# A perceiver block on one core: queries leave PSUM over both banks in one go, and a router's logits are made ahead of the norm they wait for

## The reference

```python
q = ln_lat @ Wq                                   # 16 heads of 64
kv = jnp.concatenate([xn, ln_lat], axis=1) @ Wkv
weight = jnp.einsum('bhld,bhnd->bhln', q * scale, k * scale)
weight = softmax(where(full_mask, weight, neg))   # mask in the second layer
return out @ Wout
...
logits = xf @ Wr.T + expert_bias                  # xf = rmsnorm(x1) * g2
rw = softmax(logits); topw, topi = top_k(rw, 2); topw = softmax(topw)
shared = _swiglu(xf, sW1, sW2, sW3)
specialist = einsum('te,etd->td', combine, eo)    # eo: 8 experts on xf
```

## Time and profile before

| | us |
|---|---|
| median of 3 runs | 2065.31 (2063.27 to 2069.19) |
| the profiled execution's own time | 2067.51 |
| its span in the trace | 2065.6 |
| PE busy | 1914.6 (93%) |
| DVE busy | 1682.6 (81%) |
| ACT busy | 1250.5 (61%) |
| POOL busy | 898.2 (43%) |

### The profile page before, as it was taken

One profiled execution on the slowest core, in us unless ns is written; L12 is line 12 of the kernel. 1 busy time (PEld: TensorE's weight loads), 2 busy tenths in 40 slices (PEclk: granted clock), 3 DMA queues, 4 the chain that ended last, 5 costly groups with the idle time before them and its releaser, 6 DMA issues. The chain is left out here.

```text
span 2065.6 us, 34989 instructions
## 1 busy us (share of the span) xinstructions
PE 1914.6 (93%) x12326; PEld 1037.9 (50%) x12326; DVE 1682.6 (81%) x3999; ACT 1250.5 (61%) x2237; POOL 898.2 (43%) x951
## 2 busy tenths in 40 slices
PE   7899999999999999899788999999999999998786
PEld 6444544444454544433656545454545454544585
DVE  6889889889989896699666788879797978786657
ACT  4466666665757666444244676867777777776312
POOL 5576565666666652088231424333232323232004
PEclk9899999999999999989998999999999999999898
DMA  4332222222222220132104011211121111110100
GB/s 140 89 105 65 70 67 68 67 68 68 73 73 68 51 67 1 48 115 89 40 1 126 14 38 39 50 39 38 39 59 36 41 39 39 38 30 1 29 1 10
DMA packets 148854, 110.53 MB, mean 54 GB/s; under 512 B 120892, under 2 KB 136232, under 8 KB 148680
## 3 DMA queue, kind: packets, MB, share of 16 engines
q1 hardware_dynamic: 148680, 108.31, 18.8%
HBM read 65.15 MB, written 14.29 MB: 38 GB/s over the span
## 5 line engine op out<-in xcount | busy, mean ns | idle before, releaser
L1260 DVE TENSOR_TENSOR x_p_lo<-x_psum,x_p_hi 128x512 f16<-128x512 f32 (+1 forms) x864 | 583.9, 682 | 110.6 <-ACT x_psum L1022 109.8
L1021 ACT ACTIVATE x_p_hi<-x_psum 128x512 f16<-128x512 f32 (+1 forms) x448 | 268.2, 599 | 260.3 <-PE x_psum L865 210.3
L1021 ACT ACTIVATE x_p_hi<-x_psum,x_bcol 128x512 f16<-128x512 f32 (+1 forms) x416 | 289.7, 696 | 153.9 <-PE x_psum L865 151.9
L891 PE MATMUL x_psum<-x_p_hi,x_x_both 128*128 128x512 f16 (+1 forms) x832 | 317.1, 381 | 30.4 <-DVE x_p_lo L1260 29.5
L863 PE MATMUL x_psum<-x_q,x_xT_both 128*128 128x512 f16 x832 | 316.3, 380 | 3.0 <-DMA x_q<-x_shift_rows 3.0
L892 PE MATMUL x_psum<-x_p_lo,x_x_both 128*128 128x512 f16 (+1 forms) x832 | 315.7, 379 | 0.0
L893 PE MATMUL x_psum<-x_p_hi,x_x_both 128*128 128x512 f16 (+1 forms) x832 | 315.6, 379 | 0.0
L865 PE MATMUL x_psum<-x_q,x_xT_both 128*128 128x512 f16 x832 | 315.6, 379 | 0.0
L864 PE MATMUL x_psum<-x_q,x_xT_both 128*128 128x512 f16 x832 | 315.6, 379 | 0.0
L1199 DVE CUSTOM_DVE_ANT_0 x_junk<-x_psum,x_brow 128x512 bf16<-128x512 f32 (+2 forms) x512 | 279.3, 584 | 8.8 <-PE x_psum L942 6.7
L1202 DVE TENSOR_REDUCE x_mx<-x_psum 128x1 f32<-128x512 f32 (+2 forms) x512 | 276.6, 583 | 2.2 <-PE x_psum L942 1.1
(11 more groups left out here) (486 smaller groups left out, 3609.8 us busy)
## 6 DMA issues: line engine op xcount, KB each, us to landing
x_x_both<-context_rows SPq DMA_DIRECT2D x32, 832.0 KB, 5.3
context_rows<-x_x SPq DMA_DIRECT2D x16, 832.0 KB, 3.5
x_raw<-in_ctx SPq DMA_DIRECT2D x16, 768.0 KB
ssm_c_row<-ssm_bc_rows SPq DMA_DIRECT2D x16, 512.0 KB, 4.2
ssm_b_wide<-ssm_bc_rows SPq DMA_DIRECT2D x7, 512.0 KB, 3.5
x_mrow<-in_mask_BxS_bk SPq DMA_DIRECT2D x16, 200.1 KB
x_Wkv<-in_L_xattn_Wkv SPq DMA_DIRECT2D x4, 512.0 KB, 5.3
x_xT_both<-context_rows SPq DMA_TRANSPOSE x96, 4.0
```

What stands on the lines that cost most here:

```text
L891: pe.matmul(out, v_hi, p_hi[r][rows, :], start=start, stop=False)
L1021: act.activation(p_hi[r][rows, :], score[r][rows, :], ACT.Exp, scale=SCORE_UNIT, **bias).then_inc(p_hi_ready, 1)
L1260: v.tensor_tensor(p_lo[r][rows, :], score[r][rows, :], p_hi[r][rows, :], ALU.subtract).then_inc(p_lo_ready, 1)
```

## The change

Two parts that do not touch each other.

In both attention loops a "q" item leaves `aux` as a whole: ACT waits for the item's second bank, then copies 512 columns twice instead of 256 columns four times; DVE subtracts 512 columns once instead of 256 twice. `aux_free` and `hi_ready` go up by two at the end, where they went up by one for each bank. PE's matmuls, their waits on `aux_free` and the table of items are as before.

In the expert block the turned tokens for the router come from `u`, before the norm: PE turns them in place of part of the idle work, ACT copies them times the weight vector, PE makes the logits there, and DVE multiplies the logits by the norm factor `r1` afterwards. The router's first exponential stands before `xf_hi`, the second behind it; the Silu table is loaded behind the second one instead of behind the attention's exponentials. DVE's top two come ahead of `xf_lo`, and `max_index` and the weights behind the first two `hidden`.

```diff
-                for bank in range(2):
-                    act.wait_ge(aux_ready, at.ready(item, bank))
-                    later, src = queries_part(a, bank, at.place(item), later_q, 1)
-                    act.activation(later, src, ACT.Copy, scale=Q_UNIT)
-                    high, src = queries_part(a, bank, at.place(item), q_hi, 0)
-                    act.activation(high, src, ACT.Copy, scale=Q_UNIT).then_inc(hi_ready, 1)
+                act.wait_ge(aux_ready, at.ready(item))
+                later, src = queries_part(a, at.place(item), later_q, 1)
+                act.activation(later, src, ACT.Copy, scale=Q_UNIT)
+                high, src = queries_part(a, at.place(item), q_hi, 0)
+                act.activation(high, src, ACT.Copy, scale=Q_UNIT).then_inc(hi_ready, 2)
...
-                    for bank in range(2):
-                        v.wait_ge(hi_ready, at.n * HI_PARTS + 2 * a + bank + 1)
-                        (hi, src), (lo, _) = (queries_part(a, bank, aux, q, 0) for q in (q_hi, q_lo))
-                        v.scalar_tensor_tensor(lo, src, Q_UNIT, hi, ALU.mult, ALU.subtract).then_inc(aux_free, 1)
+                    v.wait_ge(hi_ready, at.n * HI_PARTS + 2 * a + 2)
+                    (hi, src), (lo, _) = (queries_part(a, aux, q, 0) for q in (q_hi, q_lo))
+                    v.scalar_tensor_tensor(lo, src, Q_UNIT, hi, ALU.mult, ALU.subtract).then_inc(aux_free, 2)
...
-                keep_clock(pe, slot[1], ident, 28)
+                for g in range(GROUPS):
+                    pe.wait_ge(x1_ready, g + 1)
+                    for t in range(g * GT, (g + 1) * GT):
+                        ins = pe.transpose(slot[0][:, t * P:(t + 1) * P], u[:, t, :], ident[:, :])
+                    ins.then_inc(u_turned, 1)
+                keep_clock(pe, slot[1], ident, 8)
+                pe.wait_ge(uT_ready, GROUPS)
+                for t in range(NT):
+                    ins = pe.matmul(slot[2][:, t * NE:(t + 1) * NE], xfT[:, t * P:(t + 1) * P], WT[:, VR, DK:WR], start=True, stop=True)
+                ins.then_inc(lg_made, 1)
+                keep_clock(pe, slot[1], ident, 12)
...
-                    if g == GROUPS - 1:
-                        act.activation(warm[:, :], ident[:, 0:1], ACT.Silu)
...
+                for g in range(GROUPS):
+                    act.wait_ge(u_turned, g + 1)
+                    act.activation(xfT[:, g * GT * P:(g + 1) * GT * P], slot[0][:, g * GT * P:(g + 1) * GT * P], ACT.Copy, scale=vec[:, 1:2]).then_inc(uT_ready, 1)
+                act.wait_ge(rw_less, 1)
+                act.activation(rw[:, :, :], lg[:, :, :], ACT.Exp).then_inc(rw_exp, 1)
                 act.wait_ge(xf_turned, 1)
                 for c in range(2):
                     act.activation(xf_hi[:, 512 * c:512 * c + 512], psum[:, 6 + c, :], ACT.Copy, scale=vec[:, 1:2]).then_inc(xf_hi_ready, 1)
...
+                act.wait_ge(top_less, 1)
+                act.activation(col[1][:, :], col[0][:, :], ACT.Exp).then_inc(top_exp, 1)
+                act.activation(warm[:, :], ident[:, 0:1], ACT.Silu)
...
-                v.tensor_tensor(lg[:, :, :], logits, bias_r[:, :].unsqueeze(1).to_broadcast(wide), ALU.add).then_inc(lg_read, 1)
+                logits = slot[2][:, 0:NT * NE].rearrange("p (t e) -> p t e", e=NE)
+                v.tensor_tensor(lg[:, :, :], logits, r1.unsqueeze(2).to_broadcast(wide), ALU.mult).then_inc(lg_read, 1)
...
+                steps.link(v.tensor_tensor(lg[:, :, :], lg[:, :, :], bias_r[:, :].unsqueeze(1).to_broadcast(wide), ALU.add))
...
+                v.tensor_tensor(col[0][:, :], best[:, :, 1], best[:, :, 0], ALU.subtract).then_inc(top_less, 1)
...
+                hidden(0)
+                hidden(1)
                 for t in range(NT):
                     steps.mark(v.max_index(place[:, t, :], best[:, t, :], rw[:, t, :]))
```

More of the change, by code:

```diff
@@ L723, in wait_alone, with queries_part @@
         eng.wait_ge(sem, value)
-    def queries_part(a, bank, aux, q, k):
-        src = aux[:, 512 * bank:512 * bank + 512].rearrange("p (c h k l) -> p c h k l", h=2, k=2, l=L)[:, :, :, k, :]
-        c = (a % 2) * (NC_ // 2) + bank * (NC_ // 4)
+    def queries_part(a, aux, q, k):
+        src = aux.rearrange("p (c h k l) -> p c h k l", h=2, k=2, l=L)[:, :, :, k, :]
+        c = (a % 2) * (NC_ // 2)
         if k == 0:
-            dst = q[a // 2][0][:, c:c + NC_ // 4, :].rearrange("p c (h l) -> p c h l", l=L)
+            dst = q[a // 2][0][:, c:c + NC_ // 2, :].rearrange("p c (h l) -> p c h l", l=L)
         else:
-            dst = q[:, (a // 2) * HL + c * P:(a // 2) * HL + (c + NC_ // 4) * P].rearrange("p (c h l) -> p c h l", h=2, l=L)
+            dst = q[:, (a // 2) * HL + c * P:(a // 2) * HL + (c + NC_ // 2) * P].rearrange("p (c h l) -> p c h l", h=2, l=L)
         return dst, src
@@ L1655, in expert_block @@
         pT_ready_v = sem("pT_ready_v")
-        (xf_ready, xf_turned, xfT_ready, lg_made, lg_read, rw_less, rw_exp, top_less, top_exp, comb_ready) = (
-            sem(n) for n in ("xf_ready", "xf_turned", "xfT_ready", "lg_made", "lg_read", "rw_less", "rw_exp", "top_less", "top_exp", "comb_ready"))
+        (xf_ready, xf_turned, lg_made, lg_read, rw_less, rw_exp, top_less, top_exp, comb_ready) = (
+            sem(n) for n in ("xf_ready", "xf_turned", "lg_made", "lg_read", "rw_less", "rw_exp", "top_less", "top_exp", "comb_ready"))
         (up_made, gated_made, silu_ready, hid_ready, down_made, added, res_ready) = (
             sem(n) for n in ("up_made", "gated_made", "silu_ready", "hid_ready", "down_made", "added", "res_ready"))
+        u_turned, uT_ready = sem("u_turned"), sem("uT_ready")
         W_hi_ready, W_lo_ready, xf_hi_ready, xf_lo_ready, hid_hi_ready, hid_lo_ready = (
@@ L1810, in down @@
                     pe.wait_ge(hid_lo_ready, e + 1)
-                    if e == 1:
+                    if e == 0:
                         pe.wait_ge(lg_read, 1)
@@ L1830, in _ @@
                     expert(slot[1], GATED + e, gated_made)
[L1831 to L1836, removed]
+                    if e >= LATE:
                         down(e - LATE)
@@ L1878, in _ @@
                     act.activation(xf_hi[:, 512 * c:512 * c + 512], psum[:, 6 + c, :], ACT.Copy, scale=vec[:, 1:2]).then_inc(xf_hi_ready, 1)
-                for c in range(2):
-                    act.wait_ge(xf_lo_ready, c + 1)
-                    act.activation(xfT[:, 512 * c:512 * c + 512], psum[:, 6 + c, :], ACT.Copy, scale=vec[:, 1:2]).then_inc(xfT_ready, 1)
+                act.wait_ge(top_less, 1)
+                act.activation(col[1][:, :], col[0][:, :], ACT.Exp).then_inc(top_exp, 1)
+                act.activation(warm[:, :], ident[:, 0:1], ACT.Silu)
                 def high(e):
@@ L1892, in _ @@
                         high(1)
[L1893 to L1896, removed]
                     act.wait_ge(up_made, e + 1)
@@ L1966, in add @@
                     ins.then_inc(added, 1)
[L1968 to L1972, removed]
                 v.wait_ge(counted, 1)
@@ L1976, in _ @@
                 v.wait_ge(bias_in, 16)
-                logits = slot[3][:, 0:NT * NE].rearrange("p (t e) -> p t e", e=NE)
-                v.tensor_tensor(lg[:, :, :], logits, bias_r[:, :].unsqueeze(1).to_broadcast(wide), ALU.add).then_inc(lg_read, 1)
+                logits = slot[2][:, 0:NT * NE].rearrange("p (t e) -> p t e", e=NE)
+                v.tensor_tensor(lg[:, :, :], logits, r1.unsqueeze(2).to_broadcast(wide), ALU.mult).then_inc(lg_read, 1)
                 v.wait_ge(lg_read, 1)
+                steps.link(v.tensor_tensor(lg[:, :, :], lg[:, :, :], bias_r[:, :].unsqueeze(1).to_broadcast(wide), ALU.add))
                 steps.link(v.tensor_reduce(col[0][:, :], lg[:, :, :], AX.X, ALU.max))
                 v.tensor_tensor(lg[:, :, :], lg[:, :, :], col[0][:, :].unsqueeze(2).to_broadcast(wide), ALU.subtract).then_inc(rw_less, 1)
-                hidden(1)
                 v.wait_ge(rw_exp, 1)
@@ L1989, in _ @@
                 steps.wait()
+                v.tensor_tensor(col[0][:, :], best[:, :, 1], best[:, :, 0], ALU.subtract).then_inc(top_less, 1)
+                for c in range(2):
+                    v.wait_ge(xf_hi_ready, c + 1)
+                    v.scalar_tensor_tensor(xf_lo[:, 512 * c:512 * c + 512], psum[:, 6 + c, :], vec[:, 1:2], xf_hi[:, 512 * c:512 * c + 512],
+                                           ALU.mult, ALU.subtract).then_inc(xf_lo_ready, 1)
+                hidden(0)
+                hidden(1)
                 for t in range(NT):
                     steps.mark(v.max_index(place[:, t, :], best[:, t, :], rw[:, t, :]))
-                v.tensor_tensor(col[0][:, :], best[:, :, 1], best[:, :, 0], ALU.subtract).then_inc(top_less, 1)
                 steps.wait()
```

## The result

The changed kernel takes 2101.72 us (median of 4 runs, 2100.98 to 2103.39), the kernel before, run beside it, 2067.25 (2063.27 to 2071.01). The ratio is 1.0168, 95% interval 1.0146 to 1.0191: 34.5 us slower, where +30.5 and 2096 were forecast, with a range from 2082 to 2108. The two profiled executions differ by 2100.7 - 2065.6 = 35.1 us of span.

A forecast was written before the change was run, and what follows sets the result against it. PE was taken to bound the query stretches. New waits and later stretch ends in the loops, +38.7 us, and the expert block, -8.2, summed to +30.5 and a forecast of 2096 us, range 2082 to 2108.

The forecast's parts named there:

- What bounds the stretch: Query stretches of both loops: PE sets the pace, busy 9.47 and 10.00 of 10 us; ACT has 1 to 2 to spare.
- the margin of 0.6 per bank: Query items, kernel before: each bank is free some 0.6 us before PE wants it, and the change spends that.
- Rival 1: Query items: copies and subtraction free the banks in time, the wait never forms, 2057 us; chance 0.07.
- The size of a wait: Query stretches: PE waits 0.79 us for its first bank before the second, third and fourth item.
- The third wait without mask: Six unmasked stretches: 0.18 us of lateness is already there, so the third wait adds only 0.61.
- The end of a stretch: Behind each stretch's last item: the exponential starts 0.44 us later, and all of it reaches PE.
- The places ahead of the two loops: Ahead of both attention loops, where little else runs: between 0 and 0.8 us lost, taken as 0.4.
- rival 2: Rest of each pair in the loops: PE's later waits absorb the delay, about 2068 us, same time; chance 0.05.
- rival 3: Query stretches: PE's granted clock falls, one low stretch in each of 14 costs 22 us more, 2118; chance 0.06.
- The expert block: Expert block: -1.4 for table load and warm operation, +0.1 at the front, -6.9 at the fourth "gated"; -8.2 us.
- rival 4: Expert block: the front of its loop costs what the removed waits give, 2104 us; chance 0.82 together with the forecast.
- the chain from `max_index` to `comb`: Expert block, DVE: takes 2.84 us ahead of the third `hidden`, so the fourth "gated" starts 6.7 earlier.

The follow-up runs named there:

- The two half-merged kernels: Kernel before with only ACT's copies merged: 2096.55 us, ratio 1.0127; kernel before with only DVE's subtraction merged: 2085.13 us, ratio 1.0079.
- one step of shift: Kernel before with ACT's copies and DVE's subtraction of a query item one step later in their lists: 2058.85 us, ratio 0.9952.

## Why the prediction held, point by point

- *What bounds the stretch.* Right. PE set the pace, the margin of 0.6 per bank was real and was spent, and the saved ACT time bought nothing. ACT's busy time fell by 16 us where some 20 were forecast: four times 0.38 counts the overlaps of the copies twice. Rival 1 (the wait never forms) fails by the 42 waits. The rule beside it is that of larger tiles (the Trainium skill, "Advanced Engine Details and Errata", section "The Read-Write Bubble"). It did save ACT time (597 ns for 512 columns, 384 for 256), but on an engine that waits. The other rule is that breaking up an instruction can let the work end sooner where an engine isn't saturated but causes gaps on others (the Trainium skill, "Perfetto Trace Analysis", section "Optimizing Scalar/DVE Operations"). The two half-merged kernels agree: each piece given back by bank took PE's wait down, from 0.85 to 0.52 and 0.42.
- *The size of a wait.* 0.79 forecast, 0.85 measured. Copies (1.08 for 1.10) and subtraction (0.69) were as read from the rows. The step that was undersized is DVE's start behind the copy, 0.03 in the earlier trace rows and 0.10 here (1308.22 to 1308.32). Idle time of DVE doesn't set it: the trace before has 0.03 after 4.2 us idle, that with ACT's copies by bank 0.10 after 0.29. The 512 columns alone don't either: `p_lo`, as wide, starts 0.03 behind its exponential. What differs is the wait. Where the subtraction counts up by one, the trace has its wait within the instruction (all 128 before). Where it counts up by two, the trace has a wait of its own in front of it (63 of 64 in the changed kernel; at 1308.26 in the item above, a record that the timeline leaves out). No run changes the count alone. The first wait of a stretch is 0.93: ACT starts the first item 0.12 behind PE and not 0.04, and there too the trace has a wait of its own in front. Together some 3 us.
- *The third wait without mask.* 0.61 forecast, 0.66 measured.
- *The end of a stretch.* 0.44 forecast, 0.43 measured.
- *The places ahead of the two loops.* The 0.4 taken for them can't be told: in traces of kernels that change nothing there, the starts move by -0.3 to 2.6 us.
- *Nothing given back* (rival 2). Right: the delay stays constant between stretches, and the query part alone has all of its 41 us.
- *The clock* (rival 3). It stayed at 1.00 in the stretches.
- *The expert block* (rival 4). -8.2 forecast, -8.4 measured for that part alone (-11 to -5.4 by its interval), so rival 4 fails. That the sums agree is partly luck: one step failed, and a gain that was not forecast made up for it. I take the steps from the trace of the expert part alone. From ACT's first table load there to PE's first matmul on `probs` it is 5.62 where it was 7.27, 1.65 gained for 1.4. From there to the first "up" it is 19.20 where it was 20.82, 1.6 gained, and the granted clock is higher (before, then the expert part alone; columns as in the earlier trace rows):

```profile
1014.03:1034.85 20.82, 17.36 (x235) 16.11 (x235) 10.14 (x40) 4.22 (x7) 11.08 (x8) 0.84 0.01 2
1011.89:1031.09 19.20, 15.98 (x245) 14.74 (x243) 13.97 (x56) 5.83 (x10) 12.71 (x8) 1.00 0.01 3
```

  The five traces with the block as before have 0.78 to 0.84 there and 20.8 to 21.4 us, and four of the five with the new block 1.00 and 19.2; the changed kernel's own has 0.79 and 21.65. No run shows what sets this. From the first "up" to the last "down" 5.7 are gained (6.1 in the changed kernel), where 6.9, the logits' 1.85 and the late low half's -1.6 make 7.2 (the prediction takes the last two as +0.1 together, though they make -0.25). The low half is 0.9 later, less than forecast, and the wait of 5.20 went. The step that failed is the price of the chain from `max_index` to `comb`: I took its duration before, 2.84, and it takes 1066.21 - 1061.33 = 4.88 in the changed kernel, because moved ahead it meets POOL, which costs 1.8 us at the fourth "gated". The three pieces give -9.0, near the -8.4. From the last "down" to the masked loop it is 62.04 before and 62.00 in the expert part alone, so nothing is gained behind the block; in the changed kernel it is 60.82, but the ten traces lie between 60.5 and 62.3 with either block.

The Trainium skill has that collision: "SBUF — State Buffer", section "Who interferes with whom", says that a DVE instruction with two SBUF inputs contends with a GpSimd instruction that reads SBUF, and that the order of issue decides which of the two blocks. The trace agrees: POOL's second subtraction starts at 1062.69 and the comparison at 1062.80, and it takes 2.10 us where it takes 0.22 with POOL idle, ending with POOL's instruction. The trace of the kernel before had a smaller case, 64 columns that take 0.22 in the changed kernel, ending 0.09 behind POOL's work:

```profile
1046.42 0.57 DVE L1986 TENSOR_TENSOR moe_rw<-moe_rw,moe_col 128x64 f32<-128x64 f32 x1
```

## What to carry to other kernels

Where a bounding engine fills a buffer that others empty, merging their instructions over its halves saves their fixed cost and takes away the overlap: add up the relay from the last write to the first bank's return, and compare it with the time until that bank is wanted again. Work that only later steps need belongs behind the work that the next step needs, if the ring allows it; one step of shift was worth 8 us here. When a chain is moved ahead, price it by what the other engines do at its new place, not by its duration at the old one; an operation that is far over its usual duration and ends with another engine's, as L1986 did before, is a sign of what it can meet.

## What the runs showed of the hardware

A DVE operation with two SBUF inputs that was issued behind a POOL instruction with SBUF inputs ended within 0.1 us of POOL's end in three places: 128x64 took 2.10 us beside POOL's subtraction (0.22 with POOL idle) and 0.57 in the kernel before, and 128x8 took 1.02 us beside POOL's addition in the expert part alone (0.17 otherwise). DVE's `hidden` (one input in PSUM, 1.22 us) and `max_index` beside the same POOL work kept their durations.

DVE started 0.03 us behind the copy it waited for where the trace has the wait within the instruction, and 0.10 behind it where the wait is an instruction of its own; for ACT behind PE it is 0.04 and 0.10 to 0.12. Idle times from 0.1 to 5 us before the start changed neither. Why the wait stands apart in some places was not tested.
